# A fused attention and expert kernel: another order of the jobs and loads ahead of the first gate

## The chip, the cores and the metric

One NeuronCore of a Trainium2 chip runs the whole program. The metric is the device time of one execution in microseconds (us); lower is better. All data is float32.

## What is computed

Eight batches of 512 tokens, 256 features each. Every token is normalised, and the normalised tokens `xn` go two ways. Cut to what matters:

```python
xn = layernorm(x)                                 # 8 x 512 x 256
# 1: attention with decay, 16 heads of 16, chunks of 128 tokens
q, k, v = silu(xn @ Wq.T), silu(xn @ Wk.T), xn @ Wv.T
lf = cumsum(log_sigmoid(xn @ Wf.T + delta))       # within a chunk, per head
for each chunk:
    A = (q @ k.T) * exp(lf_i - lf_j), lower triangle
    o = (q * exp(lf)) @ S + A @ v
    S = exp(lf_last) * S + (k * exp(lf_last - lf)).T @ v
s = rms_norm(o) * norm_weight @ Wo.T
# 2: eight experts, each takes the 128 tokens of every batch it rates highest
gate, idx = top_k(softmax(xn @ gate_w.T), 128)
y_e = (silu(x_in @ w_gate[e].T) * (x_in @ w_up[e].T)) @ w_down[e].T     # x_in = xn[idx]
ffn = zeros; ffn[idx] += gate * y_e
out = x + s * silu(ffn)
```

## The kernel before, in words

Matrix products are made from two float32r parts of each operand, a high part (`HI`) and the remainder (`LO`), in three passes (`PASSES`: HI·HI, HI·LO, LO·HI). ScalarE (ACT) makes the high part, VectorE (DVE) or GpSimd (POOL) the low one.

`normalise` runs first (to about 27 us). `mixed` holds the rest. Each engine's program in `mixed` is a head written out by hand and then one loop over slots `u`, the same on all engines. 16 slots belong to one batch and to one expert (`SB`); the attention of batch b runs in slots 16b to 16b+15, four scores per chunk, and the expert work starts eight slots later (`AHEAD`), so that slot u holds `gate` (first product) and `up` (second) of block n = u - 8 and `down` (third) of block n - 1. Slots 0 to 7 therefore have attention alone; the first gate is in slot 8, and from there TensorE (PE) has expert work in every slot.

What stands in a slot beside that is one *job* after the gate and one after the down (tables `AFTER_GATE`, `AFTER_VALUES`, `AFTER_DOWN`, and `SPECIAL` for exceptions):

- `("k", b, m)`, `("q", b, m)`, `("v", b, m)`: half m of the keys, queries or values of batch b. A key or query half is six matmuls (L1469); ACT takes the tanh, DVE multiplies (L1217), ACT makes the high part (L1039), and SP stores it (`store_part`, L691).
- `("t", b, m)`: half of batch b's tokens turned by four transposes (L1479); ACT (L1022) and DVE (L1240) make their parts. Keys and queries of that batch need both halves.
- `("kt", b, m)`: keys of chunk m turned back (L1492) and weighed by DVE (L1223) for the state; `("u", b, m)`: the state's update (L1497).
- `("top", 0, 0)`: the router's lists turned (L1518, L1519), from which DVE makes `idx_all` (L1246 to L1258).
- `("x", e, m)`: the gathered tokens of expert e turned (L1507), into `xgt` by ACT (L1017) and DVE (L1235). The gather is four indirect DMAs on POOL (L872), which need `idx_all`.
- `("y", b, m)`: the output product of one chunk (L1514).

Nearly all jobs write the one bank `m_ps`, and each waits until the job before it has been read (`free_at`, `m_read`). `FIRST` is the list of jobs in the head, beside which DVE makes the 16 rounds of the top-k search (`top_step`, L440 to L444; `BESIDE_JOB` says how many rounds beside which job).

In the head, and beside the slots:

- Scores `scores(u)` (L1532) need the stacks of keys and queries of their chunk, which SP loads by nine DMAs (`load_keys` L698, `load_stacks` L714) from what `store_part` has stored. Four scores make a chunk; `values(ch)` (L1568) in slot 4(ch+1) closes it, and for a chunk that is not the first of its batch it also uses the queries weighed by `e_row` (L1557, waits on `qs_done`). DVE weighs them (L1293) after ACT has taken the exponential of the rows (`rows`, L1056); SP loads them by eight DMAs (`load_rows`, L670).
- A score is multiplied by a decay tile, made by ACT (`decays`, L1050) from rows that SP loads (`load_lb`, L677) and POOL masks (`mask`, L853).
- Expert weights: `load_weights(n)` (L683) on SP, high part on ACT (`weights`, L1080), low part on POOL (`low`, L858), for block n in the slot that `block_of` names.
- Normalised tokens that the gather reads must be in DRAM: `scaled(b)` on one of three engines, then `store_xn(b)` (L651). `ffn_dram` is set to zero by eight stores of `y_sb` (L790) before the first scatter.

SP issues everything in the order of its program and waits in place, so a wait on SP holds whatever stands behind it.

```python
    FIRST = [("k", 0, 0), ("k", 0, 1), ("q", 0, 0), ("q", 0, 1), ("v", 0, 0), ("v", 0, 1)]
    SPECIAL = {("gate", 1): None, ("gate", 3): None, ("down", 0): ("top", 0, 0), ("gate", 6): None,
               ("down", 6): ("x", 0, 0), ("gate", 7): ("x", 0, 1), ("down", 7): ("kt", 0, 2)}
```

## Time and profile before

| what | value |
|---|---|
| three runs | 850.10, 852.52, 849.12 us; median 850.1 us |
| the profiled execution, its own time | 847.27 us |
| its span, first to last instruction | 845.5 us |
| TensorE busy | 787.2 us, 93% |
| VectorE, ScalarE, GpSimd busy | 544.2, 498.9, 415.0 us |
| mean granted TensorE clock | 0.962 of full |
| DMA | 160.85 MB, 190 GB/s over the span |

The span is the time between the first and the last instruction of the core. A busy share is a mean over stages with different limits, so it is read together with the stretches in which TensorE is not busy. The granted clock is 1.0 at 2.4 GHz and 0.5 at 1.2 GHz. In timelines, a bracket at a row's end gives the idle time of that engine before the row and what ended it. SPq is the queue of SyncE, which only issues transfers.

### The profile page before, as it was taken

What the parts mean: (1) busy time and instruction counts of PE and PEld (TensorE: products, weight loads), DVE (VectorE), ACT (ScalarE), POOL (GpSimd) and SP (SyncE); (2) the same over time, 40 slices, a digit from 0 to 9 for tenths busy, and PEclk for the clock granted to TensorE, in tenths of its full rate; (3) what the DMA queues carried; (4) which work ended last, traced back from release to release, by engine and by line L of the source; (5) the groups of instructions that cost most, each with busy time, mean ns of one, the idle gap of its engine ahead of it and who ended that gap; (6) DMA issues with size and microseconds to landing.
All of it is one profiled execution on the core that took longest, in us unless ns stands there. A gap on an engine that the chain in (4) does not pass through costs nothing.

```text
span 845.5 us, 17332 instructions
## 1 busy us (share of the span) xinstructions
PE 787.2 (93%) x6412; PEld 679.1 (80%) x6412; DVE 544.2 (64%) x1027; ACT 498.9 (59%) x1149; POOL 415.0 (49%) x362
## 2 busy tenths in 40 slices
PE   7637999999999999999999999999999999999970
PEld 5526788888888888888888888888888888888860
DVE  6875775576565666666666675576656666566585
ACT  5693765665556655666466655665566655645432
POOL 7756554554354716463265626463355525480311
PEclk9765999999999999999999999999999999999995
DMA  8288898776567766676566757576576758671878
GB/s 276 91 281 241 292 353 194 164 202 184 164 148 188 170 206 147 169 198 194 153 150 192 182 173 160 163 191 204 164 157 190 187 165 224 168 164 30 236 244 250
DMA packets 137637, 160.85 MB, mean 190 GB/s; under 512 B 11856, under 2 KB 108624, under 8 KB 137552
## 3 DMA queue, kind: packets, MB, share of 16 engines
q1 hardware_dynamic: 124832, 142.91, 56.4%
q0 software_dynamic: 12288, 16.79, 12.3%
q8 instruction: 51, 0.84, 0.4%
q14 instruction: 34, 0.28, 0.1%
q10 hardware_dynamic: 432, 0.04, 0.0%
HBM read 117.48 MB, written 42.21 MB: 189 GB/s over the span
## 4 chain that ended last, share of the span: by engine, by line
PE 86%; POOL 3%; DMA 3%; SPq 2%; DVE 1%; ACT 1%; issue 1%; POOLq 0%
PE y_ps L1609 21%; PE g_ps L1580 21%; PE up_ps L1580 21%; PE m_ps L1469 5%; PE a_ps L1532 4%; PE o_ps L1568 3%; PE m_ps L1514 3%; PE m_ps L1487 2%; PE m_ps L1507 2%; PE o_ps L1557 1%; PE m_ps L1497 1%; DMA qk_dram<-qk_r 1%; DMA w_plain<-ffn_dram 1%; SPq L698 1%; POOL x_all L895 1%
## 5 line engine op out<-in xcount | busy, mean ns | idle before, releaser
L1609 PE MATMUL y_ps<-w_r,hid_r 128*128 128x256 f32 x1536 | 204.6, 282 | 0.7 <-DVE hid_r L1421 0.7
L1580 PE MATMUL up_ps<-xgt,w_r 128*128 128x512 f32 x768 | 205.2, 402 | 0.0
L1580 PE MATMUL g_ps<-xgt,w_r 128*128 128x512 f32 x768 | 201.5, 398 | 0.0
L1609 PEld LDWEIGHTS y_ps<-w_r,hid_r 128*128 128x128 f32 x1536 | 192.6, 190 | 1.9 <-DVE hid_r L1421 1.1
L1399 DVE SCALAR_TENSOR_TENSOR sg<-sg,g_ps 128x512 f32<-128x512 f32 x123 | 84.3, 686 | 161.6 <-ACT sg L1166 161.6
L858 POOL TENSOR_TENSOR w_r<-w_raw,w_r 128x768 fp32r<-128x768 f32 x64 | 122.8, 1918 | 105.4 <-ACT w_r L1080 105.0
L1580 PEld LDWEIGHTS up_ps<-xgt,w_r 128*128 128x128 f32 x768 | 138.4, 188 | 27.9
L1580 PEld LDWEIGHTS g_ps<-xgt,w_r 128*128 128x128 f32 x768 | 136.5, 190 | 23.4
L1166 ACT ACTIVATE sg<-g_ps 128x512 f32<-128x512 f32 x128 | 76.5, 598 | 117.5 <-PE g_ps L1580 117.5
L887 POOL DMA_INDIRECT ffn_dram<-y_sb,idx_all x64 | 103.6, 1619 | 72.1 <-DVE y_sb L1315 56.3
L853 POOL TENSOR_SCALAR_AFFINE_SELECT lb_row<-lb_row 128x1024 f32<-128x1024 f32 x62 | 76.0, 1236 | 77.3 <-DMA lb_row<-lb_tiles 77.3
L1421 DVE TENSOR_TENSOR hid_r<-up_ps,hid_r 128x512 fp32r<-128x512 f32 x128 | 88.3, 690 | 32.2 <-ACT hid_r L1188 27.2
L872 POOL DMA_INDIRECT xg<-xn_dram,idx_all x64 | 63.3, 989 | 89.7 <-PE m_ps L1507 61.7
L1188 ACT ACTIVATE hid_r<-up_ps 128x512 fp32r<-128x512 f32 x128 | 76.0, 593 | 39.4 <-DVE up_ps L1407 32.4
L1407 DVE TENSOR_TENSOR up_ps<-sg,up_ps 128x512 f32<-128x512 f32 x123 | 85.5, 695 | 10.7 <-PE up_ps L1580 7.2
L1050 ACT ACTIVATE dec_both<-lb_row,neg_lb 128x128 f32<-128x128 f32 x200 | 63.5, 395 | 10.8 <-POOL lb_row L853 10.8
L1050 ACT ACTIVATE dec_more<-lb_row,neg_lb 128x128 f32<-128x128 f32 x200 | 63.5, 395 | 0.9 <-POOL lb_row L853 0.9
L1532 PEld LDWEIGHTS a_ps<-arena,k_st 96*128 96x128 f32 x248 | 44.8, 192 | 22.8 <-DMA arena<-qk_dram 8.4
L1532 PE MATMUL a_ps<-arena,k_st 96*128 96x256 f32 x248 | 53.9, 299 | 8.0 <-DMA arena<-qk_dram 8.0
L1080 ACT ACTIVATE w_r<-w_raw 128x768 fp32r<-128x768 f32 x64 | 53.9, 842 | 1.3 <-DMA w_raw<-w_experts 1.3
L1469 PE MATMUL m_ps<-arena,attn_w 128*128 128x512 f32 x180 | 48.1, 403 | 1.4 <-PEq L187 1.4
L1067 ACT ACTIVATE small<-o_ps 128x256 f32<-128x256 f32 x32 | 12.3, 384 | 61.8 <-PE o_ps L1568 61.7
(240 smaller groups left out, 1019.2 us busy)
## 6 DMA issues: line engine op xcount, KB each, us to landing
lb_row<-lb_tiles SPq DMA_DIRECT2D x62, 512.0 KB, 4.5
w_raw<-w_experts SPq DMA_DIRECT2D x64, 384.0 KB, 3.6
qk_dram<-qk_r SPq DMA_DIRECT2D x32, 512.0 KB, 4.3
k_st<-qk_dram SPq DMA_DIRECT2D x96, 128.0 KB, 3.7
arena<-qk_dram SPq DMA_DIRECT2D x192, 64.0 KB, 3.0
x_all<-x SPq DMA_DIRECT2D x8, 512.0 KB, 9.5
xn_dram<-x_all SPq DMA_DIRECT2D x8, 512.0 KB, 5.8
e_row<-lb_tiles SPq DMA_DIRECT2D x64, 64.0 KB
```

The costliest lines, as they stand in the source:

```text
L853: pool.affine_select(out=lb_of(n), in_=lb_of(n), compare_op=ALU.is_ge, fill=MASKED, base=0, pattern=[[0, HH], [1, P]], channel_multiplier= ...
L858: pool.tensor_tensor(w_r[:, n % MI, LO, :], w_raw[n % 2][:, :], f32(w_r[:, n % MI, HI, :]), ALU.subtract).then_inc(w_lo, 1)
L887: pool.indirect_dma_start(out=ffn_dram[:, :], out_offset=bass.IndirectOffsetOnAxis(ap=idx_all[:, e, b:b + 1], axis=0), in_=y_sb[:, t, :], ...
L1050: ins = act.activation(dec_of(t)[:, j, :], lb_of(t // 2)[:, h % HH, :], ACT.Exp, bias=neg_lb[:, ch, h:h + 1])
L1166: act.activation(sg[:, :], g_ps[:, :], ACT.Tanh if n < SILU else ACT.Silu, scale=0.5 if n < SILU else 1.0)\
L1399: dve.scalar_tensor_tensor(out=sg[:, :], in0=sg[:, :], scalar=1.0, in1=g_ps[:, :], op0=ALU.add, op1=ALU.mult).then_inc(t_done, 1)
L1407: dve.tensor_tensor(up_ps[n % 2][:, :], sg[:, :], up_ps[n % 2][:, :], ALU.mult).then_inc(h_done, 1)
L1421: dve.tensor_tensor(hid_r[n % 2][:, LO, :], up_ps[n % 2][:, :], f32(hid_r[n % 2][:, HI, :]), ALU.subtract).then_inc(hl_done, 1)
L1469: mm = pe.matmul(bank[:, :], attn_w[:, wp, sec, kk, m * P:(m + 1) * P], xt[b % 2][:, xp, kk, :], start=(j == 0 and kk == 0), stop=(j == le ...
L1532: mm = pe.matmul(a_of(t)[:, 2 * j:2 * j + 2, :], k_st[ch % 2][:, r, :], q_st[ch % 2][:, r, :, :], start=(j == 0), stop=True, skip_group_ch ...
L1580: mm = pe.matmul(bank[:, :], w_r[:, m, a, at:at + P], xgt[:, b, k, half * 512:(half + 1) * 512], start=(j == 0 and k == 0), stop=(j == len ...
L1609: mm = pe.matmul(y_ps[:, j, :], hid_r[p][:, a, j * P:(j + 1) * P], w_r[:, m, b, DOWN:DOWN + D], start=(m == 0 and q == 0 and j % 2 == 0), ...
```

## The change

It gives the slots before the first gate, the head and SP's queue another order. No matmul is added or removed.

- `("kt", 0, 0)` moves into `FIRST`, `("top", 0, 0)` from behind the first score to the front of slot 0. On DVE five search rounds now stand between the last value job and that kt (9 rounds, then none, before; 4, 0, 5 now).
- The second half of the turned tokens of batch 1 moves from slot 8 to behind the down of slot 4, `("kt", 0, 2)` from slot 7 to 5, and `("k", 1, 0)` from slot 9 to 6, there in the bank `g_ps` of the gate. `("kt", 0, 1)` writes a tile of its own.
- The eight transposes of the first gathered tokens wait for each gather apart (`first_in`), and the first block's passes are HI·HI, LO·HI, HI·LO, so that only the last needs the tokens' low part.
- ACT and POOL make weight blocks 0 and 1 in slots 2 and 3 (5 and 6 before). ACT scales batch 4 in slot 2 after the weights, batch 5 in slot 5 (slots 2 and 4 before); POOL scales batch 6 in slot 6, behind a mask (slot 5 before, in front of it).
- `rows(0)` on ACT goes from slot 3 to 7, the weighing of queries on DVE from slot 5 to 7; for batch 1 from slots 10 and 12 to 18 and 19.
- On SP `store_part(0, 3)` goes ahead of `load_keys(0)`, `store_lb(1)` ahead of `load_stacks(1)`, all eight row DMAs of batch 0 behind `load_stacks(1)`, `store_xn(5)` behind `load_weights(2)`, the rows of batch 1 from slot 6 to 15, and the zeros from slots 9 to 12 to slots 11 to 14.

```diff
-    XN_STORES = {3: 4, 5: 5, 8: 6, 10: 7}
+    XN_STORES = {3: 4, 7: 5, 8: 6, 10: 7}
...
-    BESIDE_JOB = (3, 2, 2, 9, 0)
-    FIRST = [("k", 0, 0), ("k", 0, 1), ("q", 0, 0), ("q", 0, 1), ("v", 0, 0), ("v", 0, 1)]
+    BESIDE_JOB = (3, 2, 2, 4, 0, 5)
+    FIRST = [("k", 0, 0), ("k", 0, 1), ("q", 0, 0), ("q", 0, 1), ("v", 0, 0), ("v", 0, 1), ("kt", 0, 0)]
...
-    SPECIAL = {("gate", 1): None, ("gate", 3): None, ("down", 0): ("top", 0, 0), ("gate", 6): None,
-               ("down", 6): ("x", 0, 0), ("gate", 7): ("x", 0, 1), ("down", 7): ("kt", 0, 2)}
+    SPECIAL = {("gate", 0): ("top", 0, 0), ("gate", 1): None, ("gate", 3): None, ("down", 4): ("t", 1, 1),
+               ("gate", 5): ("kt", 0, 2), ("gate", 6): ("k", 1, 0), ("down", 6): ("x", 0, 0), ("gate", 7): ("x", 0, 1),
+               ("gate", 8): None, ("gate", 9): None}
...
-            m = u % SB - 2 if u >= SB else u - 5
+            m = u % SB - 2 if u >= SB else u - 2 if u < 4 else u - 5 if u >= 7 else -1
...
+                store_part(0, 3)
                 load_keys(0)
-                store_part(0, 3)
-                load_rows(0, [0])
                 store_xn(3)
                 load_stacks(0)
+                store_lb(1)
                 load_stacks(1)
-                load_rows(0, [1])
-                store_lb(1)
+                load_rows(0)
+                for n in range(4, 6):
+                    load_lb(n)
...
-                    if u == 5:
+                    if u == 6:
                         scaled(6)
...
+                        if b == 0 and half == 0:
+                            for t in range(TPB if m == 0 else 0):
+                                pe.wait_ge(first_in[t], 16)
+                                for k in range(KD):
+                                    mm = pe.transpose(up_ps[k][:, t * P:(t + 1) * P], xg[:, t, k * P:(k + 1) * P], ident[:, :])
...
+                    if n == 0:
+                        pe.wait_ge(m_read, order["k", 1, 0] + 1)
+                        pe.wait_ge(x_hi, 2)
```

TensorE, slots 4 to 8, from the first product of values to the first up. Before:

```order
L1497 MATMUL m_ps<-v_pad,kd 32x128 x8
L1532 MATMUL a_ps<-arena,k_st 128x256 x2
L1532 MATMUL y_ps<-arena,k_st 128x256 x2
L1514 MATMUL m_ps<-wo_r,ot 128x256 x6
L1532 MATMUL a_ps<-arena,k_st 128x256 x2
L1507 MATMUL up_ps<-ident,xg 128x128 x8
L1532 MATMUL y_ps<-arena,k_st 128x256 x2
L1492 MATMUL m_ps<-ident,k_f 128x128 x2
L1580 MATMUL g_ps<-xgt,w_r 128x512 x6
L1479 MATMUL m_ps<-ident,x_all 128x128 x4
L1580 MATMUL up_ps<-xgt,w_r 128x512 x6
```

Now (L1519 is the state's update, L1501 the turned tokens, L1514 the turned keys, L1491 a key half, L1532 the gathered tokens, L1563 the scores, L1615 gate and up):

```order
L1519 MATMUL m_ps<-v_pad,kd 32x128 x8
L1563 MATMUL a_ps<-arena,k_st 128x256 x2
L1501 MATMUL m_ps<-ident,x_all 128x128 x4
L1514 MATMUL m_ps<-ident,k_f 128x128 x2
L1563 MATMUL y_ps<-arena,k_st 128x256 x2
L1545 MATMUL m_ps<-wo_r,ot 128x256 x6
L1491 MATMUL g_ps<-arena,attn_w 128x512 x6
L1563 MATMUL a_ps<-arena,k_st 128x256 x2
L1532 MATMUL up_ps<-ident,xg 128x128 x8
L1563 MATMUL y_ps<-arena,k_st 128x256 x2
L1615 MATMUL g_ps<-xgt,w_r 128x512 x6
L1615 MATMUL up_ps<-xgt,w_r 128x512 x6
```

The turned tokens that stood between gate and up, and the turned keys just ahead of the gate, now stand behind the score of slot 4; one key half, six matmuls, stands ahead of the gathered tokens.

SyncE's queue, from the store of batch 2's tokens (L651, now L659) to that of batch 4. Before:

```order
L651 DMA xn_dram<-x_all 128x4x256
L698 DMA k_st<-qk_dram 32x8x128 x3
L691 DMA qk_dram<-qk_r 128x2x512
L670 DMA e_row<-lb_tiles 128x1x128 x4
L651 DMA xn_dram<-x_all 128x4x256
L714 DMA arena<-qk_dram 16x8x128 x6
L698 DMA k_st<-qk_dram 32x8x128 x3
L714 DMA arena<-qk_dram 16x8x128 x6
L670 DMA e_row<-lb_tiles 128x1x128 x4
L756 DMA lb_tiles<-ahead 128x3x128
L677 DMA lb_row<-lb_tiles 128x1024 x2
L651 DMA xn_dram<-x_all 128x4x256
```

Now:

```order
L659 DMA xn_dram<-x_all 128x4x256
L699 DMA qk_dram<-qk_r 128x2x512
L706 DMA k_st<-qk_dram 32x8x128 x3
L659 DMA xn_dram<-x_all 128x4x256
L722 DMA arena<-qk_dram 16x8x128 x6
L764 DMA lb_tiles<-ahead 128x3x128
L706 DMA k_st<-qk_dram 32x8x128 x3
L722 DMA arena<-qk_dram 16x8x128 x6
L678 DMA e_row<-lb_tiles 128x1x128 x8
L685 DMA lb_row<-lb_tiles 128x1024 x2
L659 DMA xn_dram<-x_all 128x4x256
L706 DMA k_st<-qk_dram 32x8x128 x3
```

The last query part no longer stands behind three loads of keys and no longer ahead of four row loads; all eight row loads stand behind the second stack.

ScalarE, from the gathered tokens to the first gate's tanh (L1166 before, L1179 now). Before:

```order
L1029 ACTIVATE small<-m_ps 128x256
L1080 ACTIVATE w_r<-w_raw 128x768
L1017 ACTIVATE xgt<-up_ps 128x512 x2
L1050 ACTIVATE dec_both<-lb_row,neg_lb 128x128 x4
L1080 ACTIVATE w_r<-w_raw 128x768
L1166 ACTIVATE sg<-g_ps 128x512
```

Now:

```order
L1014 ACTIVATE th<-g_ps 128x512
L1050 ACTIVATE qk_r<-k_f 128x512
L1028 ACTIVATE xgt<-up_ps 128x512 x2
L1061 ACTIVATE dec_both<-lb_row,neg_lb 128x128 x4
L1067 ACTIVATE e_row<-e_row 128x1024
L1070 ACTIVATE exp_tot<-e_row 128x2x4
L1093 ACTIVATE w_r<-w_raw 128x768
L1179 ACTIVATE sg<-g_ps 128x512
```

The key half's tanh and high part stand ahead of the gathered tokens, and the rows' exponential between the decays of slot 8 and the weights of block 2, behind which the first tanh waits.

## Rows read from the trace of the kernel before

**Rows 1.** The page, part 1: busy time, share of the span, instructions

```profile
PE 787.2 (93%) x6412; PEld 679.1 (80%) x6412; DVE 544.2 (64%) x1027; ACT 498.9 (59%) x1149; POOL 415.0 (49%) x362
```

**Rows 2.** Stretches of 2 us: busy time per engine, granted clock, DMA share, GB/s

```profile
74.00:76.00 2.00, 1.26 (x6) 1.00 (x5) 1.90 (x5) 1.55 (x3) 0.37 (x1) 0.50 1.00 380
...
86.00:88.00 2.00, 1.41 (x56) 1.14 (x47) 1.05 (x2) 1.93 (x5) 2.00 (x3) 1.00 0.54 123
```

**Rows 3.** All waits of TensorE from 88 us on: total us, times, longest

```profile
PE m_ps L1497 <- DVE arena L1240: 0.9, 1, 0.9
PE y_ps L1609 <- DVE hid_r L1421: 0.7, 1, 0.7
```

**Rows 4.** Timeline of TensorE: start us, us, operation [idle before <-releaser]

```profile
63.26 0.80 PE L1532 MATMUL a_ps<-arena,k_st 96*128 96x256 f32 x2 [8.00 <-DMA arena<-qk_dram]
...
77.31 1.91 PE L1507 MATMUL up_ps<-ident,xg 128*128 128x128 f32 x8
...
80.97 2.91 PE L1580 MATMUL g_ps<-xgt,w_r 128*128 128x512 f32 x6
...
89.21 1.56 PE L1580 MATMUL g_ps<-xgt,w_r 128*128 128x512 f32 x6
90.61 1.56 PE L1469 MATMUL m_ps<-arena,attn_w 128*128 128x512 f32 x6
...
95.76 1.56 PE L1580 MATMUL g_ps<-xgt,w_r 128*128 128x512 f32 x6
```

**Rows 5.** Timeline of VectorE, the end of the search and the first gate

```profile
58.05 0.22 DVE L1390 COPY under<-under 64x128 f32<-64x128 f32 x1
...
64.70 0.41 DVE L1246 COPY qs<-m_ps 128x256 f32<-128x256 f32 x1
...
75.88 2.65 DVE L1293 SCALAR_TENSOR_TENSOR qs<-qs,e_row 128x1024 f32<-128x1024 f32 x1
```

**Rows 6.** Timeline of ScalarE, same columns

```profile
62.26 2.06 ACT L1113 ACTIVATE x_all<-x_all,under 128x256 f32<-128x256 f32 x4
70.53 1.06 ACT L1056 ACTIVATE e_row<-e_row 128x1024 f32<-128x1024 f32 x1 [6.21 <-DMA e_row<-lb_tiles]
...
86.34 0.58 ACT L1166 ACTIVATE sg<-g_ps 128x512 f32<-128x512 f32 x1
```

**Rows 7.** Timeline of SP's queue: start and duration of the issuing, not of the transfer

```profile
46.90 4.79 SPq L698 DMA_DIRECT2D k_st<-qk_dram  x3
51.73 0.75 SPq L691 DMA_DIRECT2D qk_dram<-qk_r  x1
...
58.69 2.69 SPq L714 DMA_DIRECT2D arena<-qk_dram  x6
...
65.75 2.56 SPq L670 DMA_DIRECT2D e_row<-lb_tiles  x4
...
77.57 0.81 SPq L683 DMA_DIRECT2D w_raw<-w_experts  x1
```

**Rows 8.** Timeline of GpSimd, same columns

```profile
66.53 1.22 POOL L872 DMA_INDIRECT xg<-xn_dram,idx_all  x1 [10.65 <-DVE idx_all L1258]
...
75.63 1.82 POOL L858 TENSOR_TENSOR w_r<-w_raw,w_r 128x768 fp32r<-128x768 f32 x1 [2.49 <-ACT w_r L1080]
```

**Rows 9.** DMA to landing: L691 at 51.7, L651 at 77.1, L683 at 77.6, 86.2, later gathers

```profile
DMA to landing us min/median/max: 6.9/6.9/6.9
...
DMA to landing us min/median/max: 7.1/7.1/7.1
...
DMA to landing us min/median/max: 8.0/8.0/8.0
...
DMA to landing us min/median/max: 3.4/3.4/3.4
...
DMA to landing us min/median/max: 4.3/5.9/7.5
```

**Rows 10.** Line L1293 after 130 us: duration ns min/median/max, first and last start

```profile
L1293 DVE SCALAR_TENSOR_TENSOR qs<-qs,e_row x6: 1226/1226/1226, 210.5 to 679.1; 128x1024 f32<-128x1024 f32 x6
```

77 lines of the change are left out of this document (51 added, 26 removed).

## The prediction

> **What bounds the kernel now.** I read the page first, then the waits of TensorE (PE), then the stretches before and after the first wait-free place, and last the timelines of the engines there. The page gives PE 787.2 us busy of a span of 845.5 [rows 1], so 58 us are not PE work. The list of PE's waits from 88 us on holds only 0.9 and 0.7 us [rows 3]: behind the first gates PE is the bound until the tail, and no other engine or queue matters there. The reader is to see in these two views that a change of order can win only in the first 90 us, and that whatever PE's third gate (95.76 us [rows 4]) gains, the end gains. The sum is therefore made up to that gate.
>
> In the head PE waits 8.00 us for the first stack and starts scores at 63.26; the gathered tokens are turned at 77.31, the first gate starts at 80.97, the second at 89.21 [rows 4]. The granted clock is 0.50 in the stretch from 74 to 76 us, where PE is busy 1.26 of 2 us, and 1.00 from 86 [rows 2]. So the head's PE work is mostly paid at the half rate: the six matmuls of a gate or a key half take 1.40 us from start to start at the full rate (89.21 to 90.61 [rows 4]) and about 2.7 at the half rate, the row of 2.91 at 80.97 less the overlap of its end.
>
> **The change, part by part.** Moved operations are the same instructions; none costs more in its new place unless said.
>
> *Lists first.* The search ends at 58.05 [rows 5]. Now the turned keys' product comes next (0.4, as the 128x256 copy at 64.70), then four copies of 0.22, so the lists are ready at 59.4; two transposes at some 0.24 each (eight took 1.91 at 77.31 [rows 4]) end at 59.9. From the copy at 64.70 to the gather at 66.53 [rows 5, 8] it is 1.8 us, so the gather starts at 61.7, 4.8 us earlier. Before, the turning of the gathered tokens began 10.8 us after the first gather with no wait ahead of it; by the same distance all has landed by 72.5. A gather is known to take 4.3 to 7.5 us to land [rows 9]. PE does not get to those transposes before 75 (below), so this cover is 2.5 us, and if it were gone each microsecond would count in full. The gain of 4.8 itself is not cashed: PE's order and the first stack are late next.
>
> *The head of SP's queue.* The last query part was issued at 51.73 behind three key loads that held the queue from 46.90 for 4.79 us, and landed 6.9 us later; the stack loads start just then, at 58.69 [rows 7, 9]. Now it stands ahead of those loads. Its bounds are 0 (the transfers queued ahead of it decide) and 4.8 earlier (the issue decides). The row of 4.79 for three issues shows a queue that is full, so most of the wait is transfers: I take 1.4, the size of a 512 KB transfer in a full queue, see the weights below. The stack loads then run from 57.3 to 60.0 (2.69 [rows 7]), and the first score follows 1.9 us later as it did (61.4 to 63.26), at 61.9. Then stand the store of rows, 0.5, and the second stack, 4.3 (61.4 to 65.75): 64.8. Eight row loads at 2.56 for four [rows 7]: 69.9. From the end of the row loads (68.3) to the weights of block 2 (77.57) it was 9.3 us; a row store and a token store of 0.5 each have left that stretch: 8.3, so **these weights are issued at 78.2**, 0.6 later than before, although nothing ahead needs the rows then. They landed in 8.0 us; the 512 KB token store right ahead of them was issued at 77.1 and landed in 7.1 [rows 9], at 84.2, so 1.4 of the 8.0 came after it. That store now stands behind: 6.6, landing at 84.8. The bounds are the 3.4 of the next load [rows 9] (81.6) and the old 8.0 (86.2).
>
> *Up to the first gate.* ScalarE (ACT) ends its decays at 62.26 [rows 6] in both; then weights 0.8, scaling 2.0, weights 0.8: it takes the turned tokens at 65.8 and VectorE (DVE) has their low part at 67. Before, this step waited 6.21 us for rows until 70.53 [rows 6]. The chain through the one bank goes on, by turns PE, ACT and DVE: state update 0.8, read 0.4, second half of tokens 0.6, ACT 0.5, DVE 0.7, turned keys 0.3, read 0.4, waits of 0.05 to 0.25 between: 71.8. The output product 1.4, the key half 1.4 to 2.7, a score 0.4, eight transposes 1.1 to 1.6: 76.1 to 77.9, take 76.8. Two high parts of 0.5 follow on ACT, so the first gate can start at 77.9 (with the clock's bounds 77.2 to 79.2) against 80.97: 3.1 us earlier, with a key half (1.40) and half the tokens (0.4) already made.
>
> *From the first gate to the second.* Gate and up end at 82 to 83.3. The values behind them need the weighed queries: ACT makes the decays of slot 8 (1.2) and the rows' exponential (1.3) from 77.9 on, 80.4, and DVE weighs in 1.2 to 2.65. DVE took 2.65 us at 75.88 [rows 5], beside a GpSimd subtraction running until 77.45 [rows 8], and 1.23 in six later cases [rows 10]; at 75.88 it ended 1.1 after GpSimd's end. I take 2.0 (the two bounds' middle, since GpSimd now scales batch 6 there in pieces): 82.4. The values, the update and a score take 2.0, so PE could go on at 84.4. But ACT's order is rows, weights of block 2, tanh of the first gate: the weights land at 84.8, so tanh ends at 86.1 (0.8 and 0.5) and DVE's product at 86.7, which frees the gate's bank. **The second gate starts at 86.7 instead of 89.21: 2.5 us.** Late next is thus a load that nothing waited on before, when tanh ran at 86.34 [rows 6] for another reason, the mask behind GpSimd's scaling.
>
> *To the third gate.* The six matmuls of 90.61 are no longer there: 1.40 more, 3.9 in all. Against this, PE idles 2.3 us ahead of the second gate, and the clock that was 1.00 from 86 [rows 2] may be at the half rate there: one gate or up at 2.7 instead of 1.4, cost 1.3, bounds 0 and 2.6. I take 1.3. Sum: 3.1 us at the first gate become 2.5 at the second, plus 1.4, less 1.3, **2.6 us gained**.
>
> *After it.* The zeros move two slots back on the queue, behind a key part instead of ahead of it. What waits there is within the 0.7 of [rows 3]; taken as 0, bounds 0.7 either way. The rows and weighing of batch 1 move by seven and eight slots in a stage where PE alone is the bound and their user is five slots further; cost 0 for that cover, and 1.4 (1.23 and a start) if it were gone.
>
> **The sum.** The profiled execution took 847.27 us for a span of 845.5; it becomes 844.7. It lies 2.8 us under the median of the three runs, 850.1, which are themselves 3.4 us apart, so I forecast from the median: 847.5 us. About 0.5%, 4.25 us, is what a measurement of this kernel can tell from no change.
>
> **Rivals.**
>
> *A, the forecast,* 847.5: the weights of block 2 end last ahead of the second gate. For it: the queue's length above. Chance 0.52, its own range 846.0 to 849.3.
>
> *B, the weights are in time* (landed by 82.9), and the weighed queries end last. For it: a single load took 3.4 in the same region [rows 9]; against it: nine stack loads and 1.5 MB are just ahead. The second gate then starts at 84.8, 4.4 earlier, plus 1.4 for the key half, less 0.8 for a shorter time at the half rate: 5.0, 845.1 us. Chance 0.22. The length of the weighing decides B's size: at 2.65 it is 4.4, at 1.23 it is 5.8. The Trainium skill, page "SBUF — State Buffer", in what it says of the port pair shared by VectorE and GpSimd, has a rule against this place: a VectorE instruction with two SBUF inputs and a GpSimd one that reads SBUF do not share, the second blocks until the first has ended. By that rule the trace agrees (2.65 beside GpSimd, 1.23 without), and B would be nearer to 5.0 than to 5.8, since GpSimd's scaling runs there.
>
> *C, slower:* the queue is later than I count. Eight row loads now stand ahead of the decay rows and the weights. If the query part lands no earlier (1.4), the row loads go at 0.8 apiece instead of 0.64 because the queue is full (1.3), and the weights take the old 8.0 (1.4), they land at 88.9, the second gate starts at 90.8, 1.6 late, and with the key half and the clock the total is 1.5 us slower: 851.6. It decides from a landing at 87.4 on; each microsecond later costs one. For it: three issues that took 4.79 [rows 7]; against it: the stretch from 60 on was not full before. Chance 0.14.
>
> *D, no change in effect,* 850.0: the idle time only moves, for instance since the gathered tokens land after 78 or the clock stays at the half rate through two gates. Chance 0.12.
>
> **How the numbers follow.** Faster by over 4.25 us is most of B (0.19) and A's edge (0.05): 0.24. Slower by over 4.25 us is only C's far end and what I have not seen: 0.06. Within it: 0.70. The range reaches from beyond B's 845.1 to beyond C's 851.6, and takes in the runs' scatter: 844.0 to 852.0.
>
> **What would show it.** In the changed profile: the gather at 61.7; scores from 62; the first gate near 77.9; ACT waiting for the load of block 2 just ahead of the first tanh; PE idle some 2 us ahead of the second gate, that one near 86.7 and the third near 93; PE's waits behind it as few as before. A first gate later than 80, or a third later than 95.8, would make the prediction wrong, and so would a new wait of over 2 us anywhere from 100 us on.

## The result and the profile after

| | before | changed |
|---|---|---|
| median | 850.1 us | 843.56 us |
| lowest and highest | 849.12, 852.52 | 843.19, 844.59 |
| the profiled execution, its own time | 847.27 us | 843.7 us |
| its span | 845.5 us | 842.0 us |
| start of gate 1, 2, 3 and of the last | 80.97, 89.21, 95.76, 812.84 | 79.86, 85.78, 91.03, 808.30 |
| from the last gate's start to the end of the span | 32.7 us | 33.7 us |

The ratio of the changed kernel to the one before is 0.9916, 95% interval 0.9899 to 0.9933: 6.5 us faster, where 2.6 were forecast, and 0.44 us under the low end of the range. With the interval the gain is 5.7 to 8.6 us. The gain of 6.5 has two parts that must be kept apart. The two profiled executions differ by 3.6 us. The other 3.0 are the distance of each profiled execution from its own median: 2.8 below it before, 0.1 above it now. One execution of the run `lists_alone` below took 1134.94 us at a granted clock of 0.649; it is in none of the ratios, and the median of the other eleven is 850.50.

The page of the changed kernel, its first part (beside [rows 1]), has 2.3 us less of TensorE and the same number of instructions. No matmul went, and the mean granted clock is 0.967 instead of 0.962, so the half rate was paid less often.

```profile
PE 784.9 (93%) x6412; PEld 676.7 (80%) x6412; DVE 542.4 (64%) x1027; ACT 499.0 (59%) x1149; POOL 414.1 (49%) x362
```

All waits of TensorE from 88 us on (beside [rows 3]) are down to one:

```profile
PE y_ps L1647 <- DVE hid_r L1443: 0.7, 1, 0.7
```

The timeline of TensorE (beside [rows 4]); L1563 is a score, L1491 the key half, L1532 the gathered tokens, L1588 the values' first part, L1615 gate and up.

```profile
62.61 0.79 PE L1563 MATMUL a_ps<-arena,k_st 96*128 96x256 f32 x2 [2.83 <-DMA arena<-qk_dram]
...
74.15 2.58 PE L1491 MATMUL g_ps<-arena,attn_w 128*128 128x512 f32 x6
...
76.80 1.04 PE L1532 MATMUL up_ps<-ident,xg 128*128 128x128 f32 x8
...
79.86 1.64 PE L1615 MATMUL g_ps<-xgt,w_r 128*128 128x512 f32 x6 [1.78 <-ACT xgt L1028]
...
83.23 0.64 PE L1588 MATMUL o_ps<-qs,small 128*32 128x128 f32 x16 [0.16 <-DVE qs L1315]
...
85.78 1.64 PE L1615 MATMUL g_ps<-xgt,w_r 128*128 128x512 f32 x6 [0.16 <-DVE sg L1421]
...
91.03 1.56 PE L1615 MATMUL g_ps<-xgt,w_r 128*128 128x512 f32 x6
```

The key half runs at the half rate (2.58 us for six matmuls), the first gate already at the full one (1.64 against 2.91 before), and ahead of the second gate nothing is left but 0.16 us. The stretches (beside [rows 2]) say the same of the granted clock, the third number from the end:

```profile
74.00:76.00 2.00, 2.00 (x7) 1.61 (x7) 0.00 (x0) 0.38 (x1) 0.05 (x1) 0.50 0.90 284
76.00:78.00 2.00, 2.00 (x15) 1.73 (x13) 0.61 (x2) 0.60 (x1) 1.99 (x2) 0.91 1.05 359
86.00:88.00 2.00, 2.00 (x10) 1.58 (x10) 1.96 (x6) 2.00 (x6) 1.90 (x4) 1.00 0.62 152
```

The timeline of ScalarE (beside [rows 6]) has the 6.21 us wait for the rows no more. It takes the tokens' high parts (L1028) behind the tanh and the high part of the key half, and waits 1.51 us for the weights of block 2 ahead of the first tanh (L1179):

```profile
76.76 0.60 ACT L1014 ACTIVATE th<-g_ps 128x512 f32<-128x512 f32 x1 [1.99 <-PE g_ps L1491]
78.11 0.63 ACT L1050 ACTIVATE qk_r<-k_f 128x512 fp32r<-128x512 f32 x1 [0.75 <-DVE k_f L1234]
78.65 1.06 ACT L1028 ACTIVATE xgt<-up_ps 128x512 fp32r<-128x512 f32 x2
...
83.59 0.85 ACT L1093 ACTIVATE w_r<-w_raw 128x768 fp32r<-128x768 f32 x1 [1.51 <-DMA w_raw<-w_experts]
84.34 0.58 ACT L1179 ACTIVATE sg<-g_ps 128x512 f32<-128x512 f32 x1
```

SP's queue (beside [rows 7]): the query part, the first stack, the row store, the row loads and the weights of block 2.

```profile
47.97 0.36 SPq L699 DMA_DIRECT2D qk_dram<-qk_r  x1
...
57.14 2.67 SPq L722 DMA_DIRECT2D arena<-qk_dram  x6
59.85 0.43 SPq L764 DMA_DIRECT2D lb_tiles<-ahead  x1
...
64.97 5.06 SPq L678 DMA_DIRECT2D e_row<-lb_tiles  x8
...
77.45 0.43 SPq L691 DMA_DIRECT2D w_raw<-w_experts  x1
```

VectorE's weighing and GpSimd's first gather (beside [rows 5, 8]):

```profile
81.86 1.23 DVE L1315 SCALAR_TENSOR_TENSOR qs<-qs,e_row 128x1024 f32<-128x1024 f32 x1 [0.60 <-ACT e_row L1067]
```

```profile
61.66 1.22 POOL L883 DMA_INDIRECT xg<-xn_dram,idx_all  x1 [6.10 <-DVE idx_all L1277]
```

### The profile page after: what moved, and what is told of

It reads as the page before. It is cut to its first block, busy times and chain, and to the rows that moved or that the text cites. A ratio compares the mean times of both kernels' runs of the same rounds, so it can differ in the third digit from the quotient of the medians.

```text
span 842.0 us, 17333 instructions
## 1 busy us (share of the span) xinstructions
PE 784.9 (93%) x6412; PEld 676.7 (80%) x6412; DVE 542.4 (64%) x1027; ACT 499.0 (59%) x1149; POOL 414.1 (49%) x362
## 4 chain that ended last, share of the span: by engine, by line
PE 87%; DMA 4%; POOL 2%; DVE 1%; SPq 1%; ACT 1%; issue 0%; ACTq 0%; POOLq 0%
PE y_ps L1647 21%; PE g_ps L1615 21%; PE up_ps L1615 21%; PE m_ps L1491 4%; PE a_ps L1563 4%; PE o_ps L1599 3%; PE m_ps L1545 3%; PE m_ps L1509 2%; PE m_ps L1538 2%; DMA qk_dram<-qk_r 1%; PE o_ps L1588 1%; PE m_ps L1519 1%; DMA w_plain<-ffn_dram 1%; PE m_ps L1501 1%; DMA w_raw<-w_experts 1%; PE m_ps L1514 1%
## 5 line engine op out<-in xcount | busy, mean ns | idle before, releaser
L1615 PE MATMUL up_ps<-xgt,w_r 128*128 128x512 f32 x768 | 205.1, 402 | 0.0
L1615 PE MATMUL g_ps<-xgt,w_r 128*128 128x512 f32 x768 | 200.3, 396 | 1.9 <-ACT xgt L1028 1.8
L1615 PEld LDWEIGHTS up_ps<-xgt,w_r 128*128 128x128 f32 x768 | 138.4, 188 | 27.9
L1615 PEld LDWEIGHTS g_ps<-xgt,w_r 128*128 128x128 f32 x768 | 135.6, 189 | 25.5 <-issue 2.3
L1179 ACT ACTIVATE sg<-g_ps 128x512 f32<-128x512 f32 x128 | 76.5, 597 | 118.1 <-PE g_ps L1615 106.5
L1563 PEld LDWEIGHTS a_ps<-arena,k_st 96*128 96x128 f32 x248 | 44.8, 191 | 18.3 <-issue 6.7
L1563 PE MATMUL a_ps<-arena,k_st 96*128 96x256 f32 x248 | 53.7, 298 | 2.8 <-DMA arena<-qk_dram 2.8
L1491 PE MATMUL m_ps<-arena,attn_w 128*128 128x512 f32 x174 | 45.6, 397 | 1.4 <-PEq L187 1.4
```

The lines of the kernel that those rows point to most:

```text
L1179: act.activation(sg[:, :], g_ps[:, :], ACT.Tanh if n < SILU else ACT.Silu, scale=0.5 if n < SILU else 1.0)\
L1491: mm = pe.matmul(bank[:, :], attn_w[:, wp, sec, kk, m * P:(m + 1) * P], xt[b % 2][:, xp, kk, :], start=(j == 0 and kk == 0), stop=(j == le ...
L1563: mm = pe.matmul(a_of(t)[:, 2 * j:2 * j + 2, :], k_st[ch % 2][:, r, :], q_st[ch % 2][:, r, :, :], start=(j == 0), stop=True, skip_group_ch ...
L1615: mm = pe.matmul(bank[:, :], w_r[:, m, a, at:at + P], xgt[:, b, k, half * 512:(half + 1) * 512], start=(j == 0 and k == 0), stop=(j == len ...
```

## The experiments

Eighteen more runs were made, all but `before_again` beside the kernel before on the same chip. "Gate 3" is the start of the third gate in the run's own profile, where the prediction made its sum. Intervals are 95% intervals of the ratio to the kernel before. Two scatters are to be kept in mind: the unchanged kernel has its third gate at 95.36, 95.76 and 98.14 in three profiles, so one profile doesn't resolve differences of a microsecond or two there, and its median is 848.79 in `null_before` and 850.1 above, so medians of unlike runs that lie 1.3 us apart may be of one kernel.

| run | what it is | median, us | ratio | gate 3 |
|---|---|---|---|---|
| null_before | before itself | 848.79 | 0.9992 [0.9975, 1.0008] | 95.36 |
| before_again | before, one more profile | 852.89 | one execution | 98.14 |
| zeros_moved | before + zeros later | 848.94 | 0.9988 [0.9972, 1.0003] | 95.47 |
| before_filled | before + 28 idle transposes | 849.80 | 1.0000 [0.9986, 1.0014] | 102.13 |
| lists_alone | before + lists first | 850.66 | 1.0011 [0.9994, 1.0029] | 97.29 |
| queue_alone | before + queue, rows, zeros | 849.70 | 0.9995 [0.9981, 1.0009] | 98.38 |
| queue_and_lists | both | 848.24 | 0.9979 [0.9963, 0.9994] | 96.67 |
| changed | | 843.56 | 0.9916 [0.9899, 0.9933] | 91.03 |
| zeros_back | changed - zeros later | 844.01 | 0.9928 [0.9908, 0.9947] | 91.43 |
| undo_lists | changed - lists first | 844.49 | 0.9938 [0.9921, 0.9955] | 92.17 |
| undo_jobs | changed - three jobs moved | 845.51 | 0.9947 [0.9926, 0.9968] | 93.85 |
| undo_key_half | changed - key half moved | 846.35 | 0.9953 [0.9933, 0.9973] | 94.45 |
| weights_store_back | changed - early blocks, row store | 846.31 | 0.9947 [0.9929, 0.9965] | 92.14 |
| rows1_back | changed - rows of batch 1 later | 849.62 | 0.9988 [0.9974, 1.0002] | 94.02 |
| undo_queue | changed - SP's head | 849.69 | 0.9995 [0.9981, 1.0010] | 97.06 |
| row_store_late | changed - row store's place | 850.74 | 1.0001 [0.9989, 1.0013] | 99.50 |
| weights2_early | changed + block 2 in slot 3 | 842.19 | 0.9905 [0.9877, 0.9933] | 90.71 |
| best | + ScalarE's order | 842.85 | 0.9914 [0.9895, 0.9932] | 90.53 |
| best2 | + a store later | 841.98 | 0.9904 [0.9887, 0.9920] | 90.36 |

### The kernel before, profiled again

No edit. 

> The kernel before, unchanged, as its own rival. Chance theory: the one profiled execution (847.27 us, span 845.5) was a lucky one of a kernel whose executions scatter; the new ones lie at 849 to 852 us and the new profile shows a place where it loses 2 to 5 us against the old profile, in the first 90 us or in the tail. Rival, a constant offset: the profiling itself shortens the run by some 2.8 us, then a new profile is again near 847.3 while the timed runs are near 850.

Measured: 848.79 us, its profiled execution 847.39, the lowest of its 12 (the highest 852.07). This run doesn't decide: a new profile near 847.3 is what the rival, a constant offset, had expected, and no place that loses 2 us or more against the old profile showed. Other runs refute the rival. The profiled execution is the highest of 12 in `before_filled` (856.03) and `row_store_late` (851.89) and the highest of 11 in `queue_alone` (851.44), so profiling doesn't shorten an execution; two of the first theory's statements failed, but its core holds, that the two profiled executions were from the low end of a scatter. The third profile shows some of what the scatter is made of.

> The kernel before itself, for one more profile. The two profiled executions so far took 847.27 and 847.39 us, the other executions up to 853.4. If the scatter lies in the head (which stretches are granted at half), an execution near 850 has its third gate 2 to 3 us later than 95.8, and the same distance from that gate to the end (717 us) within 0.5 us; if it lies further on, the third gate stays within 0.5 us of 95.8 and the distance grows.

This execution took 852.89 us, its span is 851.2. TensorE:

```profile
81.69 1.64 PE L1580 MATMUL g_ps<-xgt,w_r 128*128 128x512 f32 x6
...
89.14 0.65 PE L1497 MATMUL m_ps<-v_pad,k_f 128*32 128x128 f32 x16 [2.46 <-DVE arena L1240]
...
90.05 2.36 PE L1580 MATMUL g_ps<-xgt,w_r 128*128 128x512 f32 x6
92.21 2.34 PE L1469 MATMUL m_ps<-arena,attn_w 128*128 128x512 f32 x6
...
124.03 1.70 PE L1609 MATMUL y_ps<-w_r,hid_r 128*128 128x256 f32 x12 [1.54 <-DVE hid_r L1421]
```

and ScalarE in front of that last row:

```profile
120.68 0.63 ACT L1039 ACTIVATE qk_r<-qs 128x512 fp32r<-128x512 f32 x1 [3.07 <-DMA qk_dram<-qk_r]
```

The 5.7 us over the first profile come from three places. At the third gate it is 2.4 late: 0.8 at the second gate (0.7 at the first; the wait of 2.46 instead of 0.88 behind it is nearly made up by a first gate at the full rate), and then 1.5, the second gate and the key half mostly at the half rate (2.2 from start to start instead of 1.4). At 124.03 there are 1.5 more, a wait that the other two profiles don't have: the high part of a query half waits until the part before has been stored, and zero stores stand in the queue ahead of that store. The tail takes 34.4 us from the last gate instead of 32.7. So both of the expectation's cases hold at once.

### Is the wait behind the zeros part of the gain?

```diff
-                    if AHEAD + 1 <= u < AHEAD + 1 + B // 2:
+                    if AHEAD + 3 <= u < AHEAD + 3 + B // 2:
```

> The kernel before with the eight zero stores two slots later on SyncE's queue (11 to 14 instead of 9 to 12), nothing else. The third profile of the kernel before shows TensorE idle for 1.54 us at 124.03, behind ScalarE, which waited 3.07 us for a query part to be stored while zero stores stood in the queue; the other two profiles show no such wait. Theory 'zeros': this wait is in many of the executions; the median falls by 1 to 2 us, to 848.2 to 849.2, and the highest execution comes down. Rival 'zeros count for nothing': the scatter comes from the head alone and the median stays within 0.5 us.

> The changed kernel with the zeros back in slots 9 to 12. Theory 'zeros': the wait at slot 12 returns in many executions, the median rises by 0.8 to 2 us, to 844.4 to 845.6, and the scatter grows from 1.4 us to 2 us or more. Rival 'nothing': within 0.5 us of 843.6.

Moved in the kernel before, the median falls by 1.7 us, but the interval still holds 1. Moved back in the changed kernel, the profiled execution (846.31) has the wait, and another ahead of it:

```profile
110.96 0.64 PE L1519 MATMUL m_ps<-v_pad,kd 128*32 128x128 f32 x16 [1.76 <-DVE qs L1234]
118.88 1.69 PE L1647 MATMUL y_ps<-w_r,hid_r 128*128 128x256 f32 x12 [0.95 <-DVE hid_r L1443]
```

while four of the six executions lie at 843.57 to 844.07. The wait is real and comes in some executions only. What it adds to the medians was not resolved: 1.7 us in the kernel before, 0.4 in the changed one, neither clear of the noise.

### Is it the clock?

```diff
+                    if 1 <= u < AHEAD:
+                        if u == 1:
+                            pe.wait_ge(m_read, len(FIRST))
+                        for _ in range(4):
+                            pe.transpose(g_ps[:, 0:P], ident[:, :], ident[:, :])
```

> The kernel before with four transposes of the identity that nobody reads behind each of the slots 1 to 7 on TensorE (28 matmuls into the bank of the gate, free until slot 8), nothing else. They show what the granted clock costs. Theory 'clock': with TensorE busier from 66 to 80 us the granted clock is at its full level when the first gate starts, gate and up of slot 8 take 1.6 us each instead of 2.9, the second gate comes 1 to 3 us earlier and the time is 847 to 849, with a smaller scatter than the 848 to 853 of the kernel before. Rival 'no clock': the 28 matmuls (some 3.4 us at the full rate, 6.7 at half) only delay the chain, and the time is 850 to 853.

```profile
68.36 0.60 PE L1670 MATMUL g_ps<-ident 128*128 128x128 f32 x4
...
77.26 1.05 PE L1670 MATMUL g_ps<-ident 128*128 128x128 f32 x4
...
82.67 1.08 PE L1507 MATMUL up_ps<-ident,xg 128*128 128x128 f32 x4 [4.04 <-DMA xg<-xn_dram,idx_all]
...
88.07 2.91 PE L1580 MATMUL g_ps<-xgt,w_r 128*128 128x512 f32 x6
```

Four idle transposes take 0.60 us at 68.36 and 1.05 at 77.26: the clock rose (0.97 from 68 to 70 us) and fell again (0.50 from 76 to 78), the second time behind a wait of 3.12 us at 73.60. The first gate ran at the half rate behind a wait of 4.04 us for the gathered tokens, which this execution (856.03, the highest of 12) has and which the filler could not touch. The median stayed and the scatter grew no smaller. The run is inconclusive on the price of the clock; it shows that four idle transposes per slot held the clock over neither wait.

### One part alone

`lists_alone`: `FIRST`, `BESIDE_JOB` and the list job as in the change. 

> The kernel before with only the lists turned first: kt(0,0) in the head behind the search, the router's lists turned at the front of slot 0, so that the gather starts near 61.7. Queue, rows, jobs and weights stay where they were. Theory 'rows': ScalarE still waits for the rows until 70.5, the turned tokens come no earlier, the first gate stays within 0.7 us of 81 and the time is 849 to 850.5. Theory 'lists': the first gate comes 2 to 4 us earlier and the time is 846 to 848.

`queue_alone`: SP's head, the late rows and weighing of both batches, the zeros. 

> The kernel before with only the queue part of the change: the head of SyncE's queue as in the changed kernel (last query part first, row store ahead of the second stack, all eight row loads behind it), the exponential of the rows and the weighing of the queries in slot 7, those of batch 1 in slots 18 and 19, the zeros two slots later. Lists, jobs and weight blocks stay where they were. Theory 'rows' (the 6.21 us in which ScalarE waited for the rows at 70.53 held the turned tokens and with them the whole chain through m_ps): the chain starts 3 to 4 us earlier, the first gate comes near 79, and the time falls by 2 to 3 us, to 847 to 848. Theory 'lists' (the gather at 66.5 and its landing some 10.8 us later decide, whatever the rows do): TensorE then waits for the gathered tokens until 77.3, the first gate stays within 0.5 us of 81 and the time within 1 us of 850.1.

Neither theory held of both. In `lists_alone` the gather comes early, but ScalarE stands before the rows, even longer than before, and with it the turned tokens and the chain through `m_ps`:

```profile
72.11 1.06 ACT L1056 ACTIVATE e_row<-e_row 128x1024 f32<-128x1024 f32 x1 [6.96 <-DMA e_row<-lb_tiles]
```

In `queue_alone` ScalarE is free, and TensorE waits for the gathered tokens instead; then the gate runs at the half rate and the turned tokens wait for a key tile:

```profile
77.68 1.94 PE L1515 MATMUL up_ps<-ident,xg 128*128 128x128 f32 x8 [3.08 <-DMA xg<-xn_dram,idx_all]
...
81.36 2.91 PE L1588 MATMUL g_ps<-xgt,w_r 128*128 128x512 f32 x6
85.76 1.12 PE L1487 MATMUL m_ps<-ident,x_all 128*128 128x128 f32 x4 [1.49 <-DVE kd L1228]
```

`queue_and_lists` has both. 

> The kernel before with the two parts together that did nothing alone: the queue part of queue_alone (849.7) and the lists of lists_alone (850.7). In the first TensorE waited 3.08 us for the gathered tokens to land, in the second ScalarE 6.96 us for the rows. Theory 'two covers of one wait': together neither is left, the first gate comes at 77 to 79 and the time is 846 to 848. Rival 'the jobs fill': without jobs and weights moved the second gate waits for the tanh and the state's update all the same, at half clock, and the time is 848.5 to 850.

```profile
74.70 2.55 PE L1590 MATMUL g_ps<-xgt,w_r 128*128 128x512 f32 x6
83.34 1.12 PE L1489 MATMUL m_ps<-ident,x_all 128*128 128x128 f32 x4 [6.09 <-DVE kd L1230]
84.11 2.91 PE L1590 MATMUL up_ps<-xgt,w_r 128*128 128x512 f32 x6
```

The first gate starts at 74.70, 6.3 us early, and behind it stands a new wait of 6.09: the turned tokens of slot 8 need `kt(0, 2)`, which VectorE reads behind the weighing, which waits for ScalarE's rows, which stand behind decays that wait for a mask that GpSimd makes after scaling batch 6. The median falls by 2.4 us. Both expectations were half right: neither of the two waits is left ahead of the first gate, and without the jobs moved most of the 6.3 us is lost again.

### The jobs

```diff
-    SPECIAL = {("gate", 0): ("top", 0, 0), ("gate", 1): None, ("gate", 3): None, ("down", 4): ("t", 1, 1),
-               ("gate", 5): ("kt", 0, 2), ("gate", 6): ("k", 1, 0), ("down", 6): ("x", 0, 0), ("gate", 7): ("x", 0, 1),
-               ("gate", 8): None, ("gate", 9): None}
+    SPECIAL = {("gate", 0): ("top", 0, 0), ("gate", 1): None, ("gate", 3): None, ("gate", 6): None,
+               ("down", 6): ("x", 0, 0), ("gate", 7): ("x", 0, 1), ("down", 7): ("kt", 0, 2)}
```

This is `undo_jobs`; `undo_key_half` takes only the key half back to slot 9. 

> The changed kernel with the key half, the second half of the turned tokens and the turned keys of chunk 2 back in slots 9, 8 and 7. Weights theory: second gate not earlier than 85.8, and 1.4 plus 0.4 come back, and the tokens' wait ahead of the state's update (0.9 in the kernel before): 845.4 to 846.3 us. Rival, the chain ends last: first gate 4 us earlier, 843 to 844.

> The changed kernel with the key half of batch 1 made in slot 9 again, in the shared bank. Theory that the load of block 2's weights ends last ahead of the second gate (landing at 83.6 in the changed profile): the second gate stays at 85.8, and the 1.40 us of the half come back behind it: 845.0 us against 843.6. Rival, the chain of PE, ScalarE and VectorE ends last: the first gate comes 2.4 us earlier, the second 1.5 to 2.4, the half costs 1.4 later: 842.6 to 843.5.

`undo_jobs` has the wait of `queue_and_lists` again, 5.04 us ahead of the turned tokens. `undo_key_half` is the nearest to what the prediction described, a TensorE that idles until the tanh behind the weights of block 2 is done:

```profile
86.27 2.57 PE L1613 MATMUL g_ps<-xgt,w_r 128*128 128x512 f32 x6 [2.31 <-DVE sg L1419]
88.63 2.22 PE L1489 MATMUL m_ps<-arena,attn_w 128*128 128x512 f32 x6
90.69 1.56 PE L1613 MATMUL up_ps<-xgt,w_r 128*128 128x512 f32 x6
```

Idle 2.31 us, and then the gate and the key half mostly at the half rate (granted clock 0.50 from 87 to 90 us). ScalarE waited 3.66 us for the weights of block 2 ahead of that tanh. Its third gate is 3.4 later than with the key half moved: 1.4 for the six matmuls, 0.5 at the second gate's start, and the rest, 1.5, the clock (2.36 and 2.06 from start to start instead of 1.40 each, 1.6).

### The lists, taken out

`undo_lists`: the list job behind the first score again, and the turned keys and the search rounds back where they were. 

> The changed kernel with the lists turned where they were (behind the first score, kt(0,0) in slot 0, nine search rounds then none); all else is the changed kernel. Theory 'rows': the gather at 66.5 lands by 77.3, 0.5 us behind the turning at 76.80, and the list job stands again in the chain of m_ps ahead of the tokens (about 1.5 us): the first gate comes 0.5 to 2 us later than 79.86, the time is 844.1 to 845.5. Theory 'lists': the gain goes for the most part, the time is 847 or more.

The first gate comes at 80.32, 0.5 later, and the time is 0.9 higher (844.49; its five executions, 843.37 to 845.28, overlap with the changed kernel's, so even this is hardly resolved). With everything else in place TensorE has the key half to make while the gathers land, so an early gather is worth little. Theory "rows" holds here, as to the time.

### The queue, taken out

`undo_queue`: key loads, the query part, half the rows, both stacks, the other rows, the row store. 

> The changed kernel with the old head of SyncE's queue (key loads ahead of the last query part, four row loads ahead of the first stack and four behind the second, row store behind that, the loads of decay rows 4 and 5 in slots 0 and 2); ScalarE and VectorE still take the rows in slot 7. Theory 'nobody waits': what counted was only that ScalarE no longer waits for the rows; the order on the queue itself is worth the 0.7 us by which the first score comes earlier (62.61 against 63.26), and the time is 843.8 to 844.8. Theory 'queue': loads of decay rows and the mask become late, weights of block 2 move by over 1 us, and the time is 845.5 or more.

All of the gain went. ScalarE:

```profile
71.47 0.84 ACT L1094 ACTIVATE w_r<-w_raw 128x768 fp32r<-128x768 f32 x1 [6.43 <-DMA lb_tiles<-ahead]
```

The second weight block shares its memory with what the row store reads (`weights` waits on `d_out`). In slot 6 nobody noticed. In slot 3 it takes the place of the wait for the rows, almost to the size: 6.43 for 6.21 [rows 6]. So I moved that one issue alone:

```diff
-                store_lb(1)
                 load_stacks(1)
                 load_rows(0)
+                store_lb(1)
```

> The changed kernel with one issue of SyncE's queue moved: the store of the decay rows (lb_tiles<-ahead) behind the second stack and the eight row loads instead of ahead of the second stack, so some 9 to 10 us later. The run undo_queue showed ScalarE waiting 6.43 us for this store ahead of the second weight block, whose tile shares the memory that the store reads. Theory 'row store': that single position decides; ScalarE waits until 75 to 78 us for it, the first gate comes at 84 to 88 and the time is 848 to 851. Rival 'place of all': the loss of undo_queue came from the order of all loads together (query part, stacks, row loads); then this run loses at most 2 us against 843.6, to 845.5 or less.

The wait is 7.54 us, the first gate comes at 88.75, the time is 850.74. One issue of 0.43 us, in the wrong place of the queue, costs the whole gain. Is its new place a gain, then, or a condition? In `weights_store_back` it is late and the first two blocks are made in slots 5 and 6 again:

```diff
-            m = u % SB - 2 if u >= SB else u - 2 if u < 4 else u - 5 if u >= 7 else -1
+            m = u % SB - 2 if u >= SB else u - 5
```

> The changed kernel with the row store late, as in row_store_late (850.74), and the first two weight blocks made in slots 5 and 6 as in the kernel before, so that ScalarE asks for the store's end only in slot 6. Theory 'precondition': the row store counts only because block 1 is made in slot 3; with the blocks late the chain through m_ps starts on time again, the first gate comes near 80 to 82 and the time is 844 to 847. Rival 'the store counts by itself' (through the decay rows and the mask behind it on the queue): the time stays at 848.5 or more.

846.31 us: a condition of the early blocks, and the two together bring 2.75 us. Its third gate comes at 92.14, 1.1 later than the changed kernel's; the rest is lost before the fourth, 99.60 against 96.88, where ScalarE waits 1.87 us for a mask.

### The rows of batch 1

`rows1_back`: eight loads in slot 6, exponential in slot 10, weighing in slot 12. 

> The changed kernel with the rows of batch 1 where they were: their eight loads in slot 6, exponential in slot 10, weighing in slot 12. Theory: the eight loads stand ahead of the weights of block 3 and of the later stacks and cost the queue some 2 to 5 us in slot 6; if TensorE has no reserve there it loses 0.5 to 1.5 us at the third or fourth gate, 844.1 to 845.1. Rival (the prediction's cost of 0): 843.2 to 844.0.

849.62 us, far beyond both expectations. SP's queue:

```profile
77.69 0.43 SPq L691 DMA_DIRECT2D w_raw<-w_experts  x1
80.85 5.35 SPq L678 DMA_DIRECT2D e_row<-lb_tiles  x8
...
86.75 0.60 SPq L691 DMA_DIRECT2D w_raw<-w_experts  x1
```

and ScalarE:

```profile
91.82 0.85 ACT L1091 ACTIVATE w_r<-w_raw 128x768 fp32r<-128x768 f32 x1 [4.85 <-DMA w_raw<-w_experts]
```

The loads overwrite the row tile, so SP waits until batch 0's queries are weighed. That is now in slot 7, not 5; the queue stands still for 2.7 us, then 5.35 us of loads follow, and the weights of block 3 are issued at 86.75 instead of 78.41. The fourth gate starts at 102.38 instead of 96.88.

The profile of this run shows something else. Up to slot 6 its program is the changed kernel's, and yet its first gate starts at 76.74, 3.1 us ahead of the 79.86 there. The granted clock is 0.91 already from 66 to 68 us (0.50 in the changed kernel's profile), and the key half takes 1.40 us from start to start instead of 2.41.

```profile
76.74 1.63 PE L1611 MATMUL g_ps<-xgt,w_r 128*128 128x512 f32 x6 [1.78 <-ACT xgt L1026]
...
85.65 1.90 PE L1611 MATMUL g_ps<-xgt,w_r 128*128 128x512 f32 x6 [2.28 <-DVE sg L1417]
87.35 2.76 PE L1611 MATMUL up_ps<-xgt,w_r 128*128 128x512 f32 x6
```

The second gate starts at 85.65 all the same (85.78 in the changed kernel), since ScalarE waits 3.63 us for the weights of block 2. So in this execution the forecast's idle time came, 2.28 us, and its clock term too: gate and up take 1.70 and 2.56 us from start to start instead of 1.40 each, 1.5. Part of this run's late third gate is this and not the edit.

### Beyond the change

`weights2_early` loads block 2 in slot 3, ahead of the third stack:

```diff
-                    if u in (6, 7):
-                        load_weights(u - 4)
+                    if u in (3, 7):
+                        load_weights(2 if u == 3 else 3)
```

> The changed kernel with the weights of block 2 issued ahead of the third stack, near 72.4 us instead of 77.5, so that they land by 79 and ScalarE no longer waits for them (1.5 us in the changed profile). If the weights end last ahead of the second gate, as the forecast had it, that gate comes at 84.0 instead of 85.8: 841.8 us. Rival, the values behind the weighed queries end last (TensorE waited only 0.16 us for the gate's bank in the changed profile): at most 0.3 us, 843.3.

842.19 us; the wait of 1.51 us ahead of the first tanh is gone, and the second gate starts only 0.23 earlier, because TensorE itself was busy until then. Where the other 1.1 us of the median come from stays open. `best` adds ScalarE's order: the gathered tokens ahead of the key half's high part, the rows ahead of the decays of slot 8. 

> The changed kernel with the weights of block 2 loaded in slot 3 (as in weights2_early) and, on ScalarE and VectorE, the high and low part of the key half behind the gathered tokens instead of ahead of them, the rows' exponential ahead of the decays of slot 8. ScalarE then takes the high parts of the gathered tokens as soon as they are turned: theory 'ScalarE's order is what the first gate waits for': the 1.78 us wait ahead of the first gate shrinks to about 1.0, the first gate comes near 79.1, the time is 0.8 us under weights2_early, 841.0 to 841.8. Rival: the weighed queries or the tanh then end last and the second gate stays at 85.5; the time is 842.0 to 842.5.

```profile
78.46 1.67 PE L1618 MATMUL g_ps<-xgt,w_r 128*128 128x512 f32 x6 [0.92 <-ACT xgt L1028]
...
85.02 0.50 PE L1566 MATMUL a_ps<-arena,k_st 96*128 96x256 f32 x2 [1.02 <-DMA arena<-qk_dram]
```

The wait ahead of the first gate halves, 1.78 to 0.92 us, and the gate comes 1.4 us earlier (0.9 of it by that wait), but then the third stack, behind the weights on the queue, ends last, and nothing is won. `best2` puts the token store of batch 4 behind that stack (slot 4 instead of 3):

> The run best once more with the token store of batch 4 behind the third stack (slot 4 instead of 3), 512 KB less ahead of that stack. In best the first gate came at 78.46 (79.86 in the changed kernel), but TensorE then waited 1.02 us at 85.02 for the third stack, so that the second gate stayed at 85.36. Theory 'queue': the stack lands 1.0 to 1.4 us earlier, that wait goes, the second gate comes at 84.2 to 84.6 and the time is 841.2 to 842.0. Rival: another wait (tanh, state update) ends at the same time, the second gate stays at 85.2 or later and the time is 842.3 or more.

The stack's wait is gone and the third gate comes at 90.36, but the second gate stays at 85.20: its rival held as to the trace, its theory as to the time. All three lie within 0.9 us of each other; `best2` and `weights2_early` are 1.4 to 1.6 us under the changed kernel's median, with all their executions (841.62 to 843.05) under its lowest of 843.19. They are the fastest versions that ran; the intervals of their ratios overlap with that of the changed kernel.

## Why the prediction was wrong, step by step

Two steps failed. The base of the sum took a distance between profile and median over to the changed kernel that isn't there any more (3.0 us), and the idle time and the half rate ahead of the second gate, 2.3 and 1.3 us, did not come in the changed kernel's profile (2.1 us at the third gate).

- **Behind 88 us TensorE is the bound, and the third gate's gain is the end's.** Right in kind: gates 3 to 128 keep their distance within 0.3 us. It is not quite the end's gain: 4.54 us at the last gate, 3.5 in the span, since the tail took 1.0 us longer. The three profiles of the kernel before have tails of 32.7, 33.5 and 34.4 us, so a difference of this size comes without any change.
- **Lists first.** The lists were turned from 59.12 on (forecast 59.4), the gather came at 61.66 (61.7). That most of it is not cashed was right: `undo_lists` loses 0.9.
- **SP's queue.** The query part was issued 3.8 us earlier and took 9.1 to land instead of 6.9, so it landed 1.6 earlier (forecast 1.4), and the stack loads started at 57.14 (57.3); first score 62.61 (61.9), row loads to 70.03 (69.9), block 2 issued 77.45 (78.2) and landed after 6.1 (6.6), at 83.56 (84.8). These are well sized. What I left out was what the positions are for: two of them are conditions, the row store's of the early blocks and that of batch 1's rows of the late weighing, and each alone takes the gain back (850.74 and 849.62).
- **First gate at 77.9:** it came at 79.86. Half of the 2.0 us was lost before: the transposes ended at 77.84 (forecast 76.8), with a key half near its upper bound, 2.58 us of 2.7. The other half is *"Two high parts of 0.5 follow on ACT"*: ScalarE stands behind the key half's tanh, waits 0.75 us for VectorE's product, makes the key half's high part and only then takes the tokens. `best` takes the tokens first and has the gate at 78.46, against 79.95 in `weights2_early`, from which it differs by ScalarE's and VectorE's order alone; 0.86 of that is the shorter wait. The first half is scatter in part, as `rows1_back` with its 76.74 shows.
- **Second gate at 86.7, behind the weights of block 2:** it came at 85.78. ScalarE did wait for the load, 1.51 us, but TensorE hardly waited for ScalarE, 0.16 us. Of the 2.3 us of idle time 1.2 went because TensorE was busy longer, until 85.62 instead of 84.4, since its first gate was late; 0.9 went because the load landed at 83.56 instead of 84.8, so that the gate's bank came free earlier; the rest is the 0.16.
- **Idle 2.3 us, hence 1.3 for the clock:** this term failed, and is the larger half of the miss in the trace. The granted clock is 0.91 from 76 to 78 us and 1.00 from 78 on, and the second gate and its up take 1.48 and 1.40 us from start to start. `undo_key_half` and `rows1_back` have the idle time of the forecast, 2.31 and 2.28 us, and pay 1.6 and 1.5. The mechanism was right, the condition was not met.
- **The sum at the third gate:** 2.5 + 1.4 - 1.3 = 2.6 forecast; 3.43 + 1.40 - 0.10 = 4.73 measured (the last 0.10 is 1.48 for 1.40 in the second gate, and what follows). The size is near rival B's 5.0, by luck in part: B's condition, a landing by 82.9, was not met, though as in B the values did wait last for the weighed queries (0.16 us at 83.23).
- **After it, zeros at 0:** for the changed kernel within half a microsecond. But the kernel before pays a wait of 1.5 us behind them in one of three profiles, and I took the absence from one profile for absence. **Rows of batch 1 at 0:** right as a sum, wrong as a statement on cover: left in place they would have cost 6 us.
- **The base:** *"so I forecast from the median"* carried the 2.8 us between profile and median over to the changed kernel. This is the largest single error, 3.0 of 3.9 us. That distance was no property of measuring (the profiled execution is the highest of its run in `queue_alone`, `before_filled` and `row_store_late`); it was time that other executions of the kernel before lose and the profiled one had not lost. `before_again` shows one such execution, with a wait, a half-rate pair and a longer tail. The changed kernel's executions lie within 1.4 us instead of 3.4. That the change takes away what those losses depend on is likely but argued: one support is that the second gate stands at 85.65 and 85.78 behind first gates 3.1 us apart. How the 3.0 divides between the head, the zeros and the tail stays open. The split into 2.1 at the gate and 3.0 of base also depends on which execution of the kernel before was profiled.

Together: 2.6 + 2.1 at the third gate - 1.2 up to the end of the span + 3.0 of the base = 6.5.

## What to carry to other kernels

Behind a wait that holds a chain others can stand ready to take its place. Here ScalarE waited for the rows until 70.53, with another order for the row store until 71.47, TensorE for the gathered tokens until 77.68 or for a key tile until 83.34. So a part tried alone reads as worthless (849.7, 850.7) and a part left out as worth everything (849.6 to 850.7). Before costing a moved job, ask what else its instruction waits for in the new place, memory that it shares included, and list those as conditions with their price. And profile a kernel that scatters more than once before taking its stalls from the trace: the single profile shows the waits of one execution, and a change is also worth the waits that this execution happened not to have.
